# Weights, input and output weights read from DRAM as rounded and rest parts, in a gated delta rule layer on one core

## The reference

```
qkvz = x @ W_qkvz          # per key head (16): q 128, k 128, v 2x128, z 2x128
ba   = x @ W_ba            # beta = sigmoid(b), g = -exp(A_log) * softplus(a + dt_bias)
q, k, v = silu(causal_conv(., 4 taps)); q, k = l2norm(q), l2norm(k)
per value head (32): chunked gated delta rule (a triangular system per chunk and a state that
                     passes from chunk to chunk)
o = core * silu(z); o = o * rsqrt(mean(o*o) + eps) * norm_weight
x = layernorm(x + o @ W_out)
x = layernorm(x + down(silu(up(x)) * gate(x)))   # ternary weights
```

## Time and profile before

| | |
|---|---|
| median of 3 runs | 4886.9 us (4884.82 to 4887.08) |
| the profiled execution, its own time | 4884.65 us |
| its span | 4882.9 us |
| granted TensorE clock, mean of the span | 0.982 |
| TensorE, VectorE, ScalarE, GpSimd busy | 95%, 75%, 76%, 63% |
| DMA | 230 MB, 47 GB/s over the span |

### The profile page before, as it was taken

The page is one execution under the profiler, slowest core; times in us unless marked ns, Lnnn a source line. Parts: engine busy times, 40 slices in busy tenths (PEclk is TensorE's granted clock), DMA queues, the critical chain, the costliest instruction groups (busy, mean ns, idle before and its releaser), DMA issues. The chain is left out here.

```text
span 4882.9 us, 140476 instructions
## 1 busy us (share of the span) xinstructions
PE 4634.1 (95%) x45578; PEld 3958.0 (81%) x45578; DVE 3673.0 (75%) x6752; ACT 3718.7 (76%) x10197; POOL 3057.6 (63%) x3690
## 2 busy tenths in 40 slices
PE   3599999999999999999999999999999999999587
PEld 3488888888888888888888888888888888888476
DVE  5477787777777787787778778787877878787454
ACT  1488888888888888888888888888888888888343
POOL 0466666666666666666666666666666666666143
PEclk9799999999999999999999999999999999999799
DMA  3211111111111111111111111111111111111000
GB/s 113 90 41 52 46 45 52 39 52 39 52 47 44 52 39 52 39 52 48 43 52 39 52 39 52 50 41 52 39 52 39 52 50 41 52 39 44 29 14 22
DMA packets 112100, 229.97 MB, mean 47 GB/s; under 512 B 9264, under 2 KB 24752, under 8 KB 112048
## 3 DMA queue, kind: packets, MB, share of 16 engines
q1 hardware_dynamic: 110896, 228.51, 14.4%
q10 hardware_dynamic: 1152, 0.79, 0.1%
HBM read 219.30 MB, written 9.96 MB: 47 GB/s over the span
## 5 line engine op out<-in xcount | busy, mean ns | idle before, releaser
L838 DVE SCALAR_TENSOR_TENSOR conv<-ps,cws,conv 128x511 f32<-128x511 f32 (+2 forms) x1536 | 1094.9, 741 | 73.5 <-ACT conv L731 73.5
L879 DVE CAST_PREDICATED pl<-masks,ps 128x512 f16<-128x512 uint16 x768 | 546.6, 712 | 535.5 <-PE ps L617 519.9
L529 PE MATMUL ps<-xb,wb 128*128 128x512 f32 x3072 | 843.3, 410 | 52.5 <-POOL xb L1008 49.0
L1014 POOL TENSOR_TENSOR xo<-xo,zs 128x512 f32<-128x512 f32 x256 | 327.4, 1279 | 891.3 <-DVE xo L930 891.3
L529 PEld LDWEIGHTS ps<-xb,wb 128*128 128x128 f32 x3072 | 543.7, 190 | 144.5 <-issue 48.3
L784 ACT ACTIVATE t<-ps 128x512 f16<-128x512 f32 x768 | 462.6, 602 | 171.0 <-PE ps L625 161.0
L731 ACT ACTIVATE conv<-ps,cws 128x512 f32<-128x512 f32 x512 | 349.9, 683 | 246.5 <-PE ps L529 240.0
L1008 POOL TENSOR_TENSOR wb<-wst,wb 128x512 fp32r<-128x512 f32 x384 | 491.8, 1281 | 30.9
L714 PE MATMUL ps<-wo,xt 128*128 128x256 f32 x2048 | 498.0, 386 | 3.4 <-ACT xt L817 2.6
L788 ACT ACTIVATE u<-ps 128x512 f16<-128x512 f32 x768 | 465.0, 605 | 0.0
L736 ACT ACTIVATE conv<-conv 128x512 f32<-128x512 f32 x512 | 322.4, 630 | 180.2 <-DVE conv L838 178.7
(11 more groups left out here) (161 smaller groups left out, 12201.0 us busy)
## 6 DMA issues: line engine op xcount, KB each, us to landing
wst<-in_Wqkvz SPq DMA_DIRECT2D x128, 768.0 KB, 4.8
xst<-in_xT SPq DMA_DIRECT2D x128, 512.0 KB, 5.5
wo<-wout_scratch SPq DMA_DIRECT2D x128, 256.0 KB, 5.4
gxb<-in_xT SPq DMA_DIRECT2D x8, 512.0 KB, 3.5
wout<-in_W_out SPq DMA_DIRECT2D x1, 4096.0 KB, 15.4
yacc<-in_x_tok SPq DMA_DIRECT2D x2, 2048.0 KB, 19.6
wout_scratch<-wout SPq DMA_DIRECT2D x1, 4096.0 KB, 12.5
out<-fob SPq DMA_DIRECT2D x8, 512.0 KB, 3.0
```

Of the source, the lines that this page charges most:

```text
L529: last = nc.tensor.matmul(proj_bank[c][:, :], wb[:, pw, k * WCOL + c * D:k * WCOL + (c + 1) * D], xb[:, px, k * S:(k + 1) * S], start=(i = ...
L838: nc.vector.scalar_tensor_tensor(out=conv[c][:, back:S], in0=proj_bank[c][:, 0:S - back], scalar=cws[p][:, c * TAPS + 3 - back:c * TAPS + ...
L879: nc.vector.copy_predicated(halves(pl[l], l, 0), mask[:, None, :, :].broadcast_to([128, NU, C // (4 << l), 2 << l]), packed(p_bank, l)).th ...
```

## The change

What it does, part by part:

- W and x: both are split once into rounded and rest parts and kept in DRAM (`x_dram`, `w_dram`). The gates stage splits x (8 samples, ScalarE the cast, GpSimd the rest) and the first two heads' W (16 pieces of 96 columns); in step a the piece of W that is wanted two heads later is loaded, split and stored (`load_raw`, `split`, `store_split`). `load_w`, `load_wz` and `load_x` bring both parts straight into `wb` and `xb`, with x in two buffers.
- W_out: GpSimd splits it in the gates stage in eight pieces; `out_product` makes three passes, and `x_copy` and the new `x_low` (VectorE) make the two parts of the turned output.
- Decay: the three-part rows and `decay_product` go. The exponent's row is loaded to all 128 partitions (`grow`, one broadcast DMA of 512 KB), GpSimd masks it (`mask_row`), and ScalarE takes the exponential with the column as bias, in 8 pieces of 128 columns.
- Key norm: keys and queries are no longer turned back. The queries are left unscaled and their norm enters the epsilon of the output norm. The keys' norm is written to DRAM (`store_norm`, 2 KB) and loaded as a row to all partitions (`load_norm`), and VectorE scales the transposed keys (`keys`). `key_tokens` copies the unscaled keys in token order.
- The output norm (`o_norm`) moves from VectorE to GpSimd.
- `ORDER` is written anew, and the PSUM banks are dealt out anew; `load_x` runs three steps ahead.

```diff
+            m["x_dram"] = nc.dram_tensor("x_scratch", (B, 128, 2, KT * S), f32, kind="Internal").ap()
+            m["w_dram"] = nc.dram_tensor("w_scratch", (NK, 128, 2 * KT, WCOL), f32, kind="Internal").ap()
+            m["wout_dram"] = nc.dram_tensor("wout_scratch", (NK, 128, 2, R, H), f32, kind="Internal").ap()
...
+            def load(b):
+                if b >= 2:
+                    sp.wait_ge(ba_mm.sem, b - 1)
+                    sp.wait_ge(xs_low.sem, b - 1)
+                sp.dma_start(xb[b % 2][:, :, :], io["xT"][b].rearrange("k p n -> p k n")).then_inc(x_in[b % 2].sem, 16)
+
+            def store(b):
+                sp.wait_ge(xs_low.sem, b + 1)
+                sp.dma_start(x_dram[b], xs[b % 2][:, :, :, :].bitcast(f32).rearrange("p q k n -> p q (k n)"))\
+                    .then_inc(xs_out[b % 2].sem, 16)
+
+            def load_w(f):
+                if f >= 2:
+                    sp.wait_ge(ws_low.sem, f - 1)
+                sp.dma_start(wraw[f % 2][:, :, :], w_columns(io, slice(f, f + 1))).then_inc(wraw_in[f % 2].sem, 16)
+
+            def store_w(f):
+                sp.wait_ge(ws_low.sem, f + 1)
+                at = f % B * WP
+                sp.dma_start(w_dram[f // B][:, :, at:at + WP], ws[f % 2][:, :, :, :].bitcast(f32).rearrange("p q k n -> p (q k) n"))\
+                    .then_inc(ws_out[f % 2].sem, 16)
+            load(0)
+            load(1)
+            for b in range(2, B):
+                store(b - 2)
+                load(b)
+            store(B - 2)
+            store(B - 1)
+            load_w(0)
+            load_w(1)
+            for f in range(2, AHEAD * B):
+                store_w(f - 2)
+                load_w(f)
+            store_w(AHEAD * B - 2)
+            store_w(AHEAD * B - 1)
             for dst, src in loads[FIRST:]:
                 sp.dma_start(dst, src).then_inc(more_in.sem, 16)
             rows_to_dram(sp, 0)
+            for p in range(2):
...
+        def _(pool):
+            for b in range(B):
+                pool.wait_ge(xs_high.sem, b + 1)
+                nc.gpsimd.tensor_tensor(xs[b % 2][:, 1, :, :], xb[b % 2][:, :, :], xs[b % 2][:, 0, :, :], ALU.subtract)\
+                    .then_inc(xs_low.sem, 1)
+            for f in range(AHEAD * B):
+                pool.wait_ge(wraw_in[f % 2].sem, f // 2 * 16 + 16)
+                if f >= 2:
+                    pool.wait_ge(ws_out[f % 2].sem, f // 2 * 16)
+                nc.gpsimd.tensor_copy(ws[f % 2][:, 0, :, :], wraw[f % 2][:, :, :]).then_inc(ws_high.sem, 1)
+                pool.wait_ge(ws_high.sem, f + 1)
+                nc.gpsimd.tensor_tensor(ws[f % 2][:, 1, :, :], wraw[f % 2][:, :, :], ws[f % 2][:, 0, :, :], ALU.subtract)\
+                    .then_inc(ws_low.sem, 1)
+            pool.wait_ge(wout_ready.sem, 1)
+            for i in range(WOUTS):
+                raw = wout[:, i * WH:(i + 1) * WH, :].rearrange("p (k h) n -> p k h n", h=R)
+                if i >= 2:
+                    pool.wait_ge(wout_out[i % 2].sem, 16 * (i // 2))
+                nc.gpsimd.tensor_copy(wparts[i % 2][:, :, 0, :, :], raw).then_inc(wout_high.sem, 1)
+                pool.wait_ge(wout_high.sem, i + 1)
+                nc.gpsimd.tensor_tensor(wparts[i % 2][:, :, 1, :, :], raw, wparts[i % 2][:, :, 0, :, :], ALU.subtract)\
+                    .then_inc(wout_low.sem, 1)
...
         ORDER = (
...
+            + at(-1, ("gate", g0)) + at(1, ("conv", Q, 3)) + at(-1, ("o_square", g0), ("o_rnorm", g0)) + at(-2, ("added", g1))
+            + at(1, ("project", V0)) + at(0, ("p", 3)) + at(-1, ("y_copy", 2)) + at(0, ("t_mm", 3)) + at(1, ("turn", K)) + at(-1, ("q_part", 2))
+            + at(0, ("t_copy", 3)) + at(-1, ("update_mm", 2)) + at(0, ("u_mm", 3)) + at(-1, ("o_norm", g0), ("state", 2)) + at(1, ("squares", K))
+            + at(0, ("p_mm", 4)) + at(1, ("tap", V0)) + at(0, ("p", 4)) + at(1, ("project", V1)) + at(2, ("load_w", 0)) + at(-1, ("ks_mm", 3))
+            + at(0, ("u_copy", 3)) + at(1, ("key_tokens", 0)) + at(0, ("t_mm", 4)) + at(-1, ("o_turn", g0)) + at(1, ("tap", V1))
+            + at(0, ("t_copy", 4)) + at(-1, ("x_copy", g0), ("intra_mm", 2)) + at(0, ("u_mm", 4)) + at(1, ("conv", V0, 1)) + at(-1, ("residual", 3))
+            + at(1, ("conv", V1, 1), ("rnorm", K), ("store_norm", 0), ("load_norm", 0)) + at(0, ("low", g1), ("u_copy", 4), ("p_mm", 5))
+            + at(-1, ("y", 3), ("out", 2)) + at(0, ("p", 5)) + at(-1, ("qs_mm", 3)) + at(0, ("t_mm", 5)) + at(-1, ("y_copy", 3), ("x_low", g0))
+            + at(0, ("u_mm", 5)) + at(1, ("silu", Q), ("conv", V0, 2)) + at(-1, ("q_part", 3)) + at(1, ("conv", V1, 2), ("conv", V0, 3))
+            + at(-1, ("out_mm", g0)) + at(1, ("conv", V1, 3)) + at(0, ("u_copy", 5)) + at(1, ("mask_row", g1), ("keys", 0)) + at(0, ("t_copy", 5))
+            + at(-1, ("intra_mm", 3)) + at(0, ("resid_mm", g0)) + at(1, ("turn", Q)) + at(-1, ("added", g0), ("out", 3)) + at(0, ("resid_mm", g1))
+            + at(1, ("gram", g0)) + at(-1, ("gate", g1)) + at(1, ("gram", g1)) + at(0, ("resid", g0)) + at(1, ("decay", g0), ("squares", Q),
+               ("decay", g1)) + at(2, ("load_rows", 0)) + at(1, ("system", g0)) + at(0, ("resid", g1), ("fix_mm", g0)) + at(1, ("attn", g0))
+            + at(0, ("residual", 0)) + at(1, ("project_z", g0)) + at(0, ("fix_mm", g1), ("fix", g0)) + at(1, ("project_z", g1))
+            + at(2, ("load_wz", 0)) + at(3, ("load_x", 0)) + at(0, ("fix", g1)) + at(1, ("diagonal", g0)) + at(-1, ("o_square", g1))
...
+            def load_w(a, p, _):
+                proj_mm.wait(sp, a - 1, 4)
+                sp.dma_start(w_dst[:, :, 0:S], w_dram[ds(a // B, 1)].rearrange("a p q n -> p (a q) n")[:, :, 0:S]).then_inc(w_in.sem, 16)
+
+            def load_wz(a, p, _):
+                z_mm.wait(sp, a - 1, 2)
+                sp.dma_start(w_dst[:, :, S:WCOL], w_dram[ds(a // B, 1)].rearrange("a p q n -> p (a q) n")[:, :, S:WCOL]).then_inc(wz_in.sem, 16)
+
+            def load_x(a, p, _):
+                proj_mm.wait(sp, a - 2, 4)
+                z_mm.wait(sp, a - 2, 2)
+                sp.dma_start(xb[p][:, :, :].bitcast(f32), x_dram[ds(a % B, 1)].rearrange("a p q n -> p (a q) n")).then_inc(x_in[p].sem, 16)
+
+            def load_raw(a, p, _):
+                ws_low.wait(sp, a - 1, 1)
+                sp.dma_start(wraw[:, :, :], w_columns(io, ds((a + AHEAD * B) % ITS, 1))).then_inc(wraw_in.sem, 16)
+
+            def store_split(a, p, _):
+                sp.wait_ge(ws_low.sem, ws_low.at(a, 1))
+                sp.dma_start(w_dram[ds((a // B + AHEAD) % NK, 1), :, :, ds((a % B) * WP, WP)].rearrange("a p q n -> p (a q) n"),
+                             ws[:, :, :, :].bitcast(f32).rearrange("p q k n -> p (q k) n")).then_inc(ws_out.sem, 16)
+                sp.wait_ge(ws_out.sem, ws_out.at(a, 16))
 
             def load_rows(a, p, _):
-                decay_mm.wait(sp, a - 1, 2)
-                sp.dma_start(lrow[3:6], rows_dram[ds(a, 1), 0].rearrange("a q h s -> (a q) h s")
-                             .rearrange("q h (n c) -> q h n c", n=NC)).then_inc(rows_in.sem, 16)
-                sp.dma_start(rrow[0:3], rows_dram[ds(a, 1), 1].rearrange("a q h s -> (a q) h s")
-                             .rearrange("q h (n c) -> q h n c", n=NC)).then_inc(rows_in.sem, 16)
+                decay_ready.wait(sp, a - 1, 2)
+                sp.dma_start(grow[:, :, :].rearrange("p u c -> p (u c)"), rows_dram[ds(a, 1)].rearrange("a n h i -> a (n h i)")
+                             .broadcast_to([128, NU * C])).then_inc(rows_in.sem, 16)
+
+            def store_norm(a, p, _):
+                sp.wait_ge(rnorm.sem, rnorm.at(a, 1))
+                rk_in.wait(sp, a - 1, 16)
+                sp.dma_start(rk_dram[0].rearrange("(i n) -> i n", n=NC), rn[:, :]).then_inc(rk_out.sem, 16)
+
+            def load_norm(a, p, _):
+                sp.wait_ge(rk_out.sem, rk_out.at(a, 16))
+                kq_ready.wait(sp, a - 1, 1)
+                sp.dma_start(rk[:, :], rk_dram.broadcast_to([128, S])).then_inc(rk_in.sem, 16)
...
-            def back_turn(a, p, c):
-                pe.wait_ge(normed.sem, normed.at(a, c + 1))
-                if c == K:
-                    normed.wait(pe, a, 1)
-                if c == Q:
-                    normed.wait(pe, a, 2)
-                for n in range(NC):
-                    last = nc.tensor.transpose(back_bank[c][:, n * C:(n + 1) * C], tokn[c][:, n, :], ident[:, :])
-                last.then_inc(back_mm.sem, 1)
...
+                passes = [(h, px, pw) for h in range(R) for px, pw in ((0, 0), (0, 1), (1, 0))]
                 for i in range(2):
-                    for h in range(R):
-                        last = nc.tensor.matmul(out_bank[g][:, i * H:(i + 1) * H], xt[:, unit(2 * g + i, h), :], wo[p][:, h, :],
-                                                start=(h == 0), stop=(h == R - 1))
+                    for j, (h, px, pw) in enumerate(passes):
```

(50 more changed lines are left out.)

381 lines of the change are left out of this document (184 added, 197 removed).

## The result

| | before | after |
|---|---|---|
| median | 4886.2 us (4 runs, 4884.82 to 4887.08) | 5272.07 us (4 runs, 5257.67 to 5280.0) |
| the profiled execution | 4884.65 us | 5257.67 us |
| its span | 4882.9 us | 5255.9 us |
| granted TensorE clock over the span | 0.982 | 0.912 |

The account below looks back on a forecast made before the run. TensorE's queue was taken as the bound: 4884.65 us, less 163 for the steps (1.27 us x 128: work saved, less the keys' wait, plus gaps taken back), plus 3 for the stages before, gave 4725 us; range 4540 to 4860.

Parts of the forecast that it names:

- What bounds the kernel: In the 128 delta-rule steps TensorE's own queue sets the time: busy 4353 of 4386 us, 34.17 us per step.
- TensorE's terms: Per step, removed matmul groups save 2.29 us and the output product's new form 0.40: 2.69 us less.
- The two blocks: TensorE's turns back of normalised keys and queries and its decay products, removed: 1.21 + 1.08 = 2.29 us per step.
- The wait for the keys: At gram g0 TensorE waits 2.0 us per step for the norm's DRAM round trip; bounds no wait to 4.3.
- The clock: TensorE's granted clock read as 1.00 in the steps' stretch; no cost for a slower clock in the sum.
- Gaps taken back: Half of TensorE's 1.1 us of small gaps per step is recovered during the stop: 0.55 us.
- Other engines at no cost: VectorE, ScalarE and GpSimd work per step fits into 31.5 us, ScalarE tightest (87 to 91%); costed at nothing.
- The stages before: Gates stage +5 us (bounds -10 and +40), first projection -8, first norm's round trip 6 back: net +3 us.
- B: At gram g0 the round trip costs more than TensorE saves: 3.8 us wait, 4960 us, slower; chance 0.11.
- A: At gram the norm's row is in time and TensorE never waits: 4543 to 4597 us; chance 0.34.
- D: At gram g0 GpSimd holds VectorE's key product up to 1.28 us: 3.3 us wait, 4890 us; chance 0.04.

Follow-up runs that it names:

- load_w_after_row: Changed kernel with load_w issued behind load_norm and also waiting until the norm's row has landed; 4535.07 us, ratio 0.9286 to the kernel before.
- out_float32: load_w_after_row with the output product as one float32 pass over the rounded parts, rest parts left out of the product; 4572.0 us.
- fill_wait_short: Changed kernel with 4 useless float32 products of 512 columns on TensorE in front of gram g0's wait for the keys; 4995.74 us.
- o_norm_vector: load_w_after_row with the output norm's multiplication back on VectorE instead of GpSimd, at the same places in ORDER; 4658.19 us.
- gates_early: load_w_after_row with W_out loaded ahead of the later weight pieces in the gates stage, on its own signal; 4534.2 us, ratio 0.9279.
- load_w_late: Changed kernel with one ORDER entry moved: load_w issued behind load_norm instead of ahead of store_norm; 4623.37 us, ratio 0.9462 to the kernel before.
- plain_row: Changed kernel with the key product reading the norm's row contiguously, so keys get other tokens' norms; 5070.87 us.

## Why the prediction was wrong, step by step

**What bounds the kernel.** Right. TensorE's queue sets the time before, and mostly in load_w_after_row too (99% busy; but see out_float32).

**TensorE's terms.** Right, and a little low. The two blocks are gone. A half of the output product takes 1.51 us (forecast 1.53), against 1.73 before, so the two halves save 0.44 and not 0.40 us. Per step 2.85 us go instead of 2.69. The runs don't say what the last 0.12 us is; the small gaps between groups are the nearest candidate.

**The wait for the keys.** The first step that failed, by its size. Mechanism and place are right, but the wait is 3.8 us in the step shown (3.7 on average) for a forecast of 2.0, near the upper bound of 4.3. From the end of project V1 to gram it is 2013.91 - 2002.70 = 11.2 us instead of 8.7, term by term:

| term | forecast | measured |
|---|---|---|
| load_w, and the store with it | 5.1 | 6.1 (2002.70 to 2008.79) |
| the row's load | 2.6 | 3.5 |
| the key product | 0.69 | 1.07 |
| hand-overs | 0.3 | 0.5 (the rest) |
| TensorE's work in the meantime | 6.7 | 7.4 |
| wait | 2.0 | 3.8 |

The two DMA terms came from W_out's load, at its best (2.6 us for 256 KB) and at its pace under a load ahead of it. The load of a row to 128 partitions is no faster than 3.0 us in any kernel here, and 1024 KB take 5.6. By the Trainium skill's fit for transfers issued by GpSimd (DMA: Bandwidth & Descriptors, Anatomy of one DMA) these would be 2.6 and 4.4 us; SP's transfers here measure above both. A cost taken from the best case of another transfer belongs at the lower end of the range.

**The clock.** The second step that failed, and this one outright: a term put at nothing without a reason. The sum priced a stop of TensorE at its own length. I read the granted clock of 1.00 in the stretch before as a property of the kernel, when it belongs to an engine that never stops for long. It costs 276 us. Without it the time would have been 4996: the wait's size alone turns the sign, and the clock adds as much again as the wait's error.

**Gaps taken back.** 0.55 us was too much. In fill_wait_short TensorE has 3.94 us per step without useful work in front of gram, in load_w_after_row 0.08, and the time differs by 3.6 us per step: some 0.3 us came back.

**Other engines at no cost.** Held for ScalarE: its 1024 exponential pieces take 326.4 us, 2.55 per step and just above the upper bound of 2.5, and don't hold TensorE up where the keys are in time. The output norm's place on GpSimd was put at nothing; in the new order its place on VectorE would cost 1.0 us per step, by o_norm_vector.

**The stages before.** +13.7 us instead of +3. The split of W_out takes 29.5 us on GpSimd (132.94 to 162.45), as the forecast's 30, but it begins only at 132.94, since W_out's scaling waits for the 4 MB behind W_out in SP's queue. With that wait gone, in gates_early, the stores of the rows in the same queue hold it.

**The rivals.** B had the mechanism and the place, with a wait of 3.8 us, but 4960 us, since it too left out the clock and took gaps back. A describes load_w_after_row: its 4543 to 4597 us against 4535 measured. D's 4890 did not come about: no GpSimd instruction runs beside the key product. The lock itself is real, on VectorE's side in o_norm_vector and on GpSimd's in the gates stage of the kernel after:

```profile
92.51 2.31 DVE L314 SCALAR_TENSOR_TENSOR gsoft<-gp,gsoft 128x2048 f32<-128x2048 f32 x1
92.75 2.51 POOL L352 TENSOR_TENSOR gws<-gwraw,gws 128x192 fp32r<-128x192 f32 x1
96.63 0.59 POOL L352 TENSOR_TENSOR gws<-gwraw,gws 128x192 fp32r<-128x192 f32 x1
```

The same subtraction of GpSimd takes 0.59 us, and 2.51 us when it is issued behind a VectorE operation of 2.31 us with two inputs in SBUF: it ends 0.44 us after that one. So the rule of the Trainium skill's page SBUF — State Buffer, section Who interferes with whom, holds there.

**The budget.** From 4886 to 5272: TensorE's work -365, the stop +461, the clock +276, the stage before +14. Together +386, as measured. The stop and the clock are differences of the same runs, so that they close the sum is no test; what the traces give by themselves is -365 and +14, and they make the 351 us that load_w_after_row gains. Against the forecast of 4725 the stop is 275 us above its term (1.45 us x 128 = 186), the clock 276 above nothing, the stage before 11 above, TensorE's work 21 below: 541 of the 547 us. Most of the rest is in the forecast's own sum, whose unrounded terms give 1.24 and not 1.27 us per step, 4 us. The terms that hold a stop hang on where load_w stands: 5272 - 4535 = 737 us, almost twice what the kernel lost.

**What stays open.** What decides whether a stop costs clock: stops up to 1.6 us cost none between 2000 and 3000 us of load_w_late, those of the kernel after there (3.2 to 4.1) all did, those of plain_row (2.9 to 3.7) did in 21 of 28 steps, and the length alone does not tell them apart. Storing and loading the norm from GpSimd's queue, which would free the chain from SP's order, was not tried.

## What to carry to other kernels

Before a small transfer goes on a chain that TensorE waits for, list what stands ahead of it in its queue and what is in flight on the DMA engines, and move every large transfer that isn't due yet behind it, behind its landing if need be. Price a stop of TensorE as the stop plus what runs at half clock behind it, and doubt a trace of a kernel without stops as a source for that price. When a change bundles a real saving with a new wait, the loss says nothing about the saving: 365 us of gain lay under this one.

## What the runs showed of the hardware

- A store of 2 KB lands 1.4 us after its issue when nothing is in front of it, 5.1 us behind 1024 KB in the same queue, and 3.8 us with those 1024 KB in another queue (medians).
- Behind a stop of 3.8 us TensorE's granted clock is 0.50 for 3.57 us and 0.77 for 4.35 us. Stops up to 1.6 us cost no clock. Eight instructions of no use in the stop (3.65 us) keep it at 1.00.
- A product of VectorE over 128x512 float32 takes 1070 ns with one operand in steps of 16 bytes, and 692 ns with it contiguous.
- A product of VectorE over 128x512 float32 with both inputs in SBUF takes 0.69 us, and 1.65 us when a GpSimd subtraction of the same size began 0.1 to 0.3 us before it (o_norm_vector, 122 cases). A GpSimd subtraction over 128x192 takes 0.59 us, and 2.51 us behind a VectorE operation of 2.31 us.
- With 56 more instructions in gram g0, the instruction queue moved 570 packets instead of 35 and TensorE stood up to 4.6 us inside a group; 14 more left it at 36.
